# Gathering a decoder's chosen tokens on TensorE: transpositions with a permutation against fp32 products

## The chip, the core and the metric

The kernel runs on one core of one Trainium2 chip. The core has TensorE (PE, matrix products into PSUM), VectorE (DVE), ScalarE (ACT), GpSimd (POOL) and SyncE (SP), which here issues the DMA transfers. The metric is the device time of one execution in microseconds, less is better; a time is the median of several runs.

## The reference

Two decoder layers on 32 sequences of 100 tokens with 256 features, each sub-block followed by a layer norm: an agent attention, a cross attention on a context of 361 rows, an attention over chosen tokens, a windowed self attention, a second cross attention, and a quantised linear layer. The change touches the third:

```
gate = sigmoid(x @ Wg)                 # one number per token
_, idx = top_k(gate, 50)               # half of the 100 tokens
attn_in = x[idx]
q, k, v = attn_in @ Wq, attn_in @ Wk, attn_in @ Wv     # 16 heads of 16
o = softmax(q k^T / 4) v @ Wo
out = zeros; out[idx] = o * gate[idx]
x = layernorm(x + out)
```

## The kernel before

Sequences are worked on in pairs (NB = 2, so 200 tokens), 16 pairs in all. Four streams A to D hold a pair each, with tiles and two PSUM banks of their own (`bk[0]`, `bk[1]`), and take four turns (TURNS = 4). Each stream goes through the stages mix, first (cross attention), pick (the chosen tokens), local, second and quant. For each engine, a generator per stream issues a short piece of work and yields; the strings in `ORDER` say, letter by letter, whose piece comes next. So each engine works through a fixed list in which the four streams are interleaved, and waits on semaphores that the other engines raise. Ahead of the turns comes a stage over all sequences (`tensor_agents` and its like), which transposes all tokens at L355.

The stage pick in `tensor_turns`, `scalar_turns` and `vector_turns` goes like this, for one pair:

- DVE forms the gate logits (L1008), ACT the exponential (L748), DVE the gates (L1012, L1014): one column of 100 for each sequence.
- PE spreads the gates of a sequence over 100 partitions, so that each token sees all gates in its row: L514, a product of the gate column, broadcast to 100 columns, with the identity.
- DVE counts, for each token, the gates above its own (and equal ones of earlier tokens): its rank, 0 to 99 (L1019, L1023). Then it compares the rank with `slots` (L1027). `slots` has 128 columns for a sequence: those of its own half hold 0 to 49, all others -1. The result `pick` is a 100x128 matrix with a one where a token goes to a slot; slots of the first sequence are columns 0 to 49, of the second 64 to 113.
- PE gathers: L521 multiplies the tokens (100x128 of a feature half c, as weights) by `pick`, sums both sequences in PSUM, and so has the chosen tokens as columns. L525 transposes `pick` (for the way back).
- ACT copies the gathered columns to `xT` (L751 in the code; the trace gives all such copies the helper's line, L693) and the transposed `pick` to `pickT`.
- PE projects to q and k (L436) and v (L540), forms the scores of 16 heads (L557), transposes the exponentials (L566, 8 for a pair) and the spread reciprocals (L581, 2 for a pair), forms the head outputs (L577) and the output projection (L441), and scatters the rows back by products with `pickT` (L589). DVE multiplies by the gate and adds the residual (L1076).

An fp32 matrix product is issued as one call and stands in the trace as two matmuls; a transposition (`e.transpose`) stands as one. L431 is the transposition of tokens that opens the other stages, L471 and L632 are transpositions of exponentials (L632, 32 for a pair), L478 is the product with the context.

Of the kernel before, what the change touches and what calls it, by code (L numbers as in the profile page):

```python
# [9 lines left out]
ALU = mybir.AluOpType  # L10
# [3 lines left out]
B, S, D, S2 = 32, 100, 256, 361  # L14
H, DH = 16, 16
P = 128
NC = D // P
NB = 2
T = NB * S
# [4 lines left out]
CAP = S // 2  # L24
assert NB * CAP == S
HALF = P // NB
# [94 lines left out]
def program(nc, ins, out):  # L121
    ctx = ExitStack()
    with ctx:
        def sb(name, shape, dt=F32):
            return ctx.enter_context(nc.sbuf_tensor(name, list(shape), dt))
# [9 lines left out]
        ident = sb("ident", [P, P])  # L135
# [1 line left out]
        ones = sb("ones", [P, S])  # L137
        minus_half = sb("minus_half", [P, NB])
        before = sb("before", [S, S])
        slots = sb("slots", [S, NB, P])  # L140
        own = sb("own", [P, 2])
        heads = sb("heads", [P, 4])
        band_w = sb("band_w", [NM, S], BF16)
# [17 lines left out]
        class Stream:  # L161
            def __init__(s, n):
                s.n, s.name = n, "ABCD"[n]
                s.x = sb(f"x{n}", [P, NB, D])
                s.ctx = sb(f"ctx{n}", [P, NB, S2C, D])
                s.ctxT = sb(f"ctxT{n}", [P, NB, NC, S2])
                s.res = sb(f"res{n}", [P, NB, D])
                s.xplus = sb(f"xplus{n}", [P, NB, D])

                s.work = sb(f"work{n}", [P, HQ * S + NB * D])  # L170
                s.prod = s.work[0:S, HQ * S:HQ * S + NB * D].rearrange("p (b d) -> p b d", b=NB)
                s.p = s.work[0:S, 0:NB * S2C * P].rearrange("p (b k) -> p b k", b=NB)
                s.e = s.work[0:S, 0:HQ * S].rearrange("p (h k) -> p h k", h=HQ)
                s.e_pick = s.work[:, 0:H * HALF].rearrange("p (n j k) -> p n j k", n=H // 2, j=2)
                s.fo = s.work[:, HQ * S:HQ * S + D]
                s.rspread_pick = s.work[:, H * HALF:H * HALF + D]
                s.yq = s.work[0:S, 0:D].bitcast(BF16).rearrange("p (b d) -> p b d", b=NB)

                s.eT = sb(f"eT{n}", [P, HQ * S])
                s.pT = s.eT[:, 0:NB * S2C * S].rearrange("p (b j t) -> p b j t", b=NB, j=S2C)  # L180
                s.agent = s.eT[0:S, HQ * S - NB * D:].rearrange("p (b d) -> p b d", b=NB)
                s.yT = s.eT[:, 0:T].bitcast(BF16)[:, 0:NC * T].rearrange("p (c t) -> p c t", c=NC)
                s.tie = s.eT[0:S, 0:T].rearrange("p (b t) -> p b t", b=NB)
                s.pick = s.eT[0:S, T:T + NB * P].rearrange("p (b m) -> p b m", b=NB)
                s.xT = sb(f"xT{n}", [P, NC, T])
                s.aT = sb(f"aT{n}", [P, NC, T])
                s.qT = sb(f"qT{n}", [P, NC, T])
                s.kT = sb(f"kT{n}", [P, 2, NC, T])


                k_rows = s.kT[:, :, :, :].rearrange("p j c t -> p (j c t)")
                s.keys = [k_rows[:, 0:4 * S], s.work[:, HQ * S:HQ * S + 4 * S], k_rows[:, 4 * S:8 * S],
                          s.res[:, :, :].rearrange("p b d -> p (b d)")[:, 0:4 * S]]
                s.lm = s.kT[0:S, :, :, :].rearrange("p j c t -> p (j c t)")[:, 0:NB * S2].rearrange("p (b k) -> p b k", b=NB)
                s.v = sb(f"v{n}", [P, NB, H, 2 * DH])
                s.v_pick = sb(f"vs{n}", [P, NB, H // 2, 2 * DH])
                s.pickT = sb(f"pickT{n}", [P, NB, S])
                s.qbias = sb(f"qb{n}", [S, NB])
                s.bn = sb(f"bn{n}", [S, NB, 6])
                s.mv = sb(f"mv{n}", [S, NB, 2])  # L200
                s.vare = sb(f"ve{n}", [S, NB])
                s.rstd = sb(f"rstd{n}", [S, NB])
                s.mx = sb(f"mx{n}", [P, H])
                s.den = sb(f"den{n}", [P, H])
                s.rden = sb(f"rden{n}", [P, H])
                s.nbias = sb(f"nb{n}", [S, NB])
                s.sum = sb(f"sum{n}", [S, NB])
                s.rsum = sb(f"rsum{n}", [S, NB])
                s.z = sb(f"z{n}", [S, NB])
                s.ez = sb(f"ez{n}", [S, NB])  # L210
                s.gp = sb(f"gp{n}", [S, NB])
                s.gate = sb(f"gate{n}", [S, NB])

                s.shift = s.ez
                s.nmean = s.gp
                s.rank = sb(f"rank{n}", [S, NB])
                s.ms = sb(f"ms{n}", [S, NB])
                s.rms = sb(f"rms{n}", [S, NB])
                s.amax = sb(f"am{n}", [S, NB])
                s.am2 = sb(f"am2{n}", [S, NB])  # L220
                s.sc = sb(f"sc{n}", [S, NB])
                s.os = sb(f"os{n}", [S, NB])
                s.load_x = Loaded(sem(f"load_x{n}"), 1)
                s.load_agent = Loaded(sem(f"load_agent{n}"), 1)
                s.load_ctx = Loaded(sem(f"load_ctx{n}"), 2)
                s.load_mask = Loaded(sem(f"load_mask{n}"), 2)
                s.stored = Loaded(sem(f"stored{n}"), 1)
                s.tensor, s.scalar, s.vector, s.gpsimd = (
                    {stage: Steps(sem(f"{engine}_{stage}{n}"), names) for stage, names in stages.items()}
                    for engine, stages in (("tensor", TENSOR), ("scalar", SCALAR), ("vector", VECTOR), ("gpsimd", GPSIMD)))  # L230
# [60 lines left out]
        ld_w0, ld_wk, ld_c, ld_first, ld_const = (sem(n) for n in ("ld_w0", "ld_wk", "ld_c", "ld_first", "ld_const"))  # L291
# [130 lines left out]
        def tensor_turns(e, s):  # L422
            bk = [psum[:, NB * s.n + b, :] for b in range(NB)]
# [68 lines left out]
            for t in range(TURNS):  # L492
# [18 lines left out]
                    e.wait_ge(ld_const, LD_CONST)  # L511
                e.wait_ge(*dve("gt", t))
                for b in range(NB):
                    last = e.matmul(bk[0][0:S, b * S:(b + 1) * S], s.gate[:, b:b + 1].to_broadcast([S, S]), ident[0:S, 0:S],  # L514
                                    start=True, stop=True)
                last.then_inc(*pe.up("gates"))
                yield
                e.wait_ge(*dve("pk1", t))
                for c in range(NC):
                    for b in range(NB):  # L520
                        last = e.matmul(bk[0][:, c * P:(c + 1) * P], s.x[0:S, b, c * P:(c + 1) * P], s.pick[:, b, :],  # L521
                                        start=b == 0, stop=b == NB - 1)
                last.then_inc(*pe.up("gath"))
                for b in range(NB):
                    last = e.transpose(bk[1][:, b * S:(b + 1) * S], s.pick[:, b, :], ident[0:S, 0:S])  # L525
                last.then_inc(*pe.up("selT"))
                yield
                e.wait_ge(*act("xT", t))
# [57 lines left out]
                yield  # L586
                e.wait_ge(*act("fo", t))
                for b in range(NB):
                    e.matmul(bk[b][0:S, 0:D], s.pickT[HALF * b:HALF * (b + 1), b, :], s.fo[HALF * b:HALF * (b + 1), :],  # L589
                             start=True, stop=True).then_inc(*pe.up(f"sc{b}"))  # L590
                yield

# [96 lines left out]
        def scalar_turns(e, s):  # L689
            bk = [psum[:, NB * s.n + b, :] for b in range(NB)]  # L690

            def copy(dst, src, **kw):
                return e.activation(dst, src, ACT.Copy, **kw)  # L693
# [46 lines left out]
            for t in range(TURNS):  # L740
# [7 lines left out]
                e.activation(s.ez[:, :], s.z[:, :], ACT.Exp, scale=-1.0).then_inc(*act.up("ez"))  # L748
                yield
                e.wait_ge(*pe("gath", t))  # L750
                copy(s.xT[:, :, 0:P], bk[0][:, 0:NC * P].rearrange("p (c m) -> p c m", c=NC)).then_inc(*act.up("xT"))  # L751
                e.wait_ge(*pe("selT", t))
                copy(s.pickT[:, :, :].rearrange("p b t -> p (b t)"), bk[1][:, 0:T]).then_inc(*act.up("selT"))
                yield
# [4 lines left out]
                e.wait_ge(*pe("v", t))  # L759
                if t == 0:  # L760
                    e.wait_ge(*s.gpsimd["start"]("zeros"))
                copy(s.v_pick[0:HALF, :, :, 0:DH],
                     bk[0][0:HALF, 0:NB * P].rearrange("p (b n d) -> p b n d", b=NB, d=DH)).then_inc(*act.up("vs0"))
                yield
                for g in range(2):
                    e.wait_ge(*dve(f"su{g}", t))
# [160 lines left out]
        def vector_turns(e, s):  # L927
# [48 lines left out]
            for t in range(TURNS):  # L976
# [47 lines left out]
                                           ALU.is_gt, ALU.add, accum_out=s.rank[:, b:b + 1]).then_inc(*dve.up(f"rk{b}"))  # L1024
                for b in range(NB):
                    e.wait_ge(*dve(f"rk{b}", t))
                    e.tensor_scalar(s.pick[:, b, :], slots[:, b, :], s.rank[:, b:b + 1], None, ALU.is_equal).then_inc(  # L1027
                        *dve.up(f"pk{b}"))
                yield
                e.wait_ge(*pe("k", t))  # L1030
# [6 lines left out]
                e.wait_ge(*pe("v", t))  # L1037
                if t == 0:
                    e.wait_ge(*s.gpsimd["start"]("zeros"))
                e.tensor_copy(s.v_pick[HALF:P, :, :, DH:2 * DH],  # L1040
                              bk[0][HALF:P, 0:NB * P].rearrange("p (b n d) -> p b n d", b=NB, d=DH)).then_inc(*dve.up("vs1"))
                yield
                e.wait_ge(*pe("hs", t))
                def of_bank(stat, g):
# [241 lines left out]
        def sync_first(e):  # L1286
# [34 lines left out]
            for n, tile in (("ident_b", ident_b), ("before", before), ("own", own), ("heads", heads), ("band_w", band_w),  # L1321
                            ("band_x", band_x)):
                e.dma_start(tile[:, :], ins[n]).then_inc(ld_const, 16)
            e.dma_start(slots[:, :, :], ins["slots"]).then_inc(ld_const, 16)
            e.wait_ge(*agent_pe("u"))
            for s in (SC_, SD):
                load_ctx(e, s, 0)
# [110 lines left out]
def constants():  # L1438

    bf = mybir.dt.np(BF16)  # L1440
    t = np.arange(S)
    edge = np.concatenate([np.arange(NEDGE), np.arange(S - NEDGE, S)])
    one_key = (edge[:, None] == t[None, :]).astype(np.float32)
    mask = np.where(np.abs(edge[:, None] - edge[None, :]) > BAND, NEG, 0.0).astype(np.float32)
    slots = np.full((S, NB, P), -1.0, np.float32)
    for b in range(NB):
        slots[:, b, b * HALF:b * HALF + CAP] = np.arange(CAP)
    return {
        "ident": np.eye(P, dtype=np.float32), "ident_b": np.eye(P).astype(bf),
        "before": (t[None, :] < t[:, None]).astype(np.float32), "slots": slots,  # L1450
# [62 lines left out]
```

## Time and profile before

| | |
|---|---|
| median of 3 runs | 916.03 us (913.7, 916.03, 917.0) |
| span of the profiled execution | 917.6 us; what lies around it is not recorded |
| mean granted TensorE clock | 0.956 |
| busy: PE, DVE, ACT, POOL | 834.6, 674.2, 491.1, 361.5 us |
| PE matmuls | 7963 |
| moved by DMA | 53.34 MB, mean 58 GB/s |

The profiled execution's span lies 1.6 us above the median of the runs. Busy time of an engine is the time in which at least one of its instructions is under way; matmuls overlap, so their mean length (some 250 ns) is not what one costs. What one costs is read from where the next group begins, which is how the chain of waits counts a piece. "PEld" is the loading of weights, which runs beside the matmuls.

### The profile page before, as it was taken

Reading aid. Unit: us, or ns where it says so; the run is one execution under the profiler, and the core shown is the slowest. Engines: PE = TensorE matmul, PEld = TensorE weight load, DVE = VectorE, ACT = ScalarE, POOL = GpSimd, SP = SyncE. Lnnn points to the kernel's source line nnn. Section 1 sums busy time; section 2 is a strip of 40 time slices with the busy share of each in tenths; the row PEclk is TensorE's granted clock in tenths of the full one; section 3 lists DMA queues with packets and bytes.
Section 4 is the critical chain, followed back from the end, with each engine's and each line's share of the span. In section 5 each row is a group of like instructions: output and inputs, shape, how many; then the busy total and the mean of one; then the engine's idle time right before and its main releaser. Section 6 shows DMA issues by size and latency. Waiting matters only on the chain.

```text
span 917.6 us, 20617 instructions
## 1 busy us (share of the span) xinstructions
PE 834.6 (91%) x7963; PEld 629.7 (69%) x7963; DVE 674.2 (73%) x1973; ACT 491.1 (54%) x1509; POOL 361.5 (39%) x592
## 2 busy tenths in 40 slices
PE   8999999997879999998886699999889899999993
PEld 5567887675657787665665588766667688866772
DVE  5255887878776788796575678788678678788676
ACT  3135455765554544685454544577446454477654
POOL 0376222027756312215654632302567621210555
PEclk9989999999998999999998799999889799999996
DMA  7880000002262000001343000001142300000001
GB/s 231 265 319 24 1 2 1 2 27 68 74 218 84 10 2 1 1 2 52 101 179 118 19 10 2 1 2 27 53 160 98 108 10 2 1 2 2 2 1 36
DMA packets 22942, 53.34 MB, mean 58 GB/s; under 512 B 3656, under 2 KB 9548, under 8 KB 22844
## 3 DMA queue, kind: packets, MB, share of 16 engines
q1 hardware_dynamic: 22844, 52.02, 16.9%
q8 instruction: 63, 1.03, 0.5%
q14 instruction: 35, 0.29, 0.1%
HBM read 48.71 MB, written 3.31 MB: 57 GB/s over the span
## 4 chain that ended last, share of the span: by engine, by line
PE 47%; DVE 8%; POOL 7%; ACT 6%; DMA 3%; issue 2%; SPq 0%; ACTq 0%; DVEq 0%; POOLq 0%
PE psum L436 8%; PE psum L441 7%; PE psum L478 5%; PE psum L621 4%; PE psum L464 4%; PE psum L641 3%; PE psum L632 3%; POOL rstd L1190 2%; DMA out<-xplus 2%; ACT x L699 2%; PE psum L624 2%; PE psum L540 1%; PE psum L557 1%; PE psum L566 1%; PE psum L521 1%
## 5 line engine op out<-in xcount | busy, mean ns | idle before, releaser
L699 ACT ACTIVATE x<-res,ez,rstd 100x256 f32<-100x256 f32 x160 | 87.5, 597 | 76.7 <-POOL ez L1193 76.4
L478 PE MATMUL psum<-eT,ctx 128*128 128x100 f32 x768 | 103.7, 293 | 8.0 <-ACT eT L693 6.0
L478 PEld LDWEIGHTS psum<-eT,ctx 128*128 128x128 f32 x768 | 99.4, 208 | 11.7 <-ACT eT L693 6.2
L1188 POOL TENSOR_SCALAR ve<-mv 100x2 f32<-100x2 f32 x96 | 21.9, 228 | 182.1 <-DVE mv L936 178.3
L464 PE MATMUL psum<-ctxT,qT 128*100 128x361 f32 x256 | 88.9, 493 | 3.7 <-ACT qT L715 3.0
L801 ACT ACTIVATE work<-psum,mx 100x100 f32<-100x100 f32 x256 | 68.1, 366 | 32.3 <-DVE mx L1099 32.0
L1190 POOL TENSOR_TENSOR rstd<-ve,minus_half 100x2 f32<-100x2 f32 x96 | 75.2, 783 | 8.0
L693 ACT ACTIVATE eT<-psum 100x400 f32<-100x400 f32 (+3 forms) x128 | 61.1, 494 | 28.7 <-PE psum L471 13.1
L1172 POOL TENSOR_TENSOR kT<-cell,kT 100x722 f32<-100x722 f32 x12 | 20.6, 1716 | 135.1 <-ACT cell L673 135.1
L933 DVE BATCH_NORM_STATS2 bn<-res 100x6 f32<-100x256 f32 x192 | 71.2, 412 | 0.0
L807 ACT ACTIVATE work<-psum,mx 100x100 f32<-100x100 f32 x256 | 69.2, 390 | 2.8 <-DVE mx L1102 2.8
L693 ACT ACTIVATE xT<-psum 128x400 f32<-128x400 f32 (+2 forms) x80 | 35.9, 448 | 63.2 <-PE psum L521 26.5
L464 PEld LDWEIGHTS psum<-ctxT,qT 128*100 128x100 f32 x256 | 43.5, 176 | 36.1 <-issue 4.9
L632 PE MATMUL psum<-ident,work 100*100 100x100 f32 x512 | 61.6, 253 | 3.3 <-ACT work L807 2.8
L632 PEld LDWEIGHTS psum<-ident,work 100*100 100x100 f32 x512 | 48.6, 128 | 13.0 <-ACT work L807 5.3
L1109 DVE RECIPROCAL xT<-psum 128x100 f32<-128x100 f32 x64 | 49.6, 775 | 9.7 <-PE psum L641 8.6
L1193 POOL TENSOR_SCALAR ez<-mv,rstd 100x1 f32<-100x1 f32 x192 | 52.1, 287 | 9.5
L1099 DVE TENSOR_REDUCE mx<-psum 100x4 f32<-100x400 f32 x64 | 36.5, 570 | 19.7 <-PE psum L624 18.7
L471 PE MATMUL psum<-ident,work 100*128 100x100 f32 x192 | 28.0, 264 | 18.6 <-ACT work L728 17.9
L1207 POOL COPY work<-rden 128x256 f32<-128x256 f32 x16 | 6.3, 396 | 95.8 <-DVE rden L1061 95.8
L471 PEld LDWEIGHTS psum<-ident,work 100*128 100x128 f32 x192 | 21.1, 147 | 27.6 <-ACT work L728 24.8
L1106 DVE COPY eT<-psum 100x400 f32<-100x400 f32 x64 | 35.7, 564 | 5.5 <-PE psum L632 5.3
(241 smaller groups left out, 2087.0 us busy)
## 6 DMA issues: line engine op xcount, KB each, us to landing
ctx<-in_ctx SPq DMA_DIRECT2D x16, 768.0 KB, 7.6
ctxT<-in_ctxT SPq DMA_DIRECT2D x16, 722.0 KB, 5.7
cell<-in_cell SPq DMA_DIRECT2D x12, 282.0 KB
seq<-in_seq SPq DMA_DIRECT2D x12, 282.0 KB
x<-in_x SPq DMA_DIRECT2D x16, 200.0 KB
out<-xplus SPq DMA_DIRECT2D x16, 200.0 KB
eT<-agent_rows SPq DMA_DIRECT2D x12, 200.0 KB
work<-in_x SPq DMA_DIRECT2D x4, 400.0 KB
```

The lines of the kernel that those rows point to most:

```text
L436: last = e.matmul(dst, w[:, c, h * P:(h + 1) * P], n(c), start=c == 0, stop=c == NC - 1)
L441: last = e.matmul(dst, xT(c), w[:, c, :], start=c == 0, stop=c == NC - 1)
L464: last = e.matmul(bk[b][0:S, 0:S2], s.qT[:, c, b * S:(b + 1) * S], s.ctxT[:, b, c, :], start=c == 0, stop=c == NC - 1)
L478: last = e.matmul(bk[b][:, c * S:(c + 1) * S], s.ctx[:, b, j, c * P:(c + 1) * P], s.pT[:, b, j, :], start=j == 0, stop=j == S2C - 1)
L632: last = e.transpose(bk[g][0:S, q * S:(q + 1) * S], s.e[:, 4 * g + q, :], ident[0:S, 0:S])
L693: return e.activation(dst, src, ACT.Copy, **kw)
L699: e.activation(dst[0:S, b, :], s.res[0:S, b, :], ACT.Identity, scale=s.rstd[:, b:b + 1], bias=s.shift[:, b:b + 1]).then_inc(*act.up(f"x{b}"))
L801: last = e.activation(s.e[:, h, :], bk[0][0:S, h % 4 * S:(h % 4 + 1) * S], ACT.Exp, bias=s.mx[0:S, h:h + 1])
L807: last = e.activation(s.e[:, h, :], bk[1][0:S, h % 4 * S:(h % 4 + 1) * S], ACT.Exp, bias=s.mx[0:S, h:h + 1])
L933: e.bn_stats(s.bn[:, b, :], s.res[0:S, b, :]).then_inc(*dve.up(f"bn{b}"))
L1190: e.tensor_tensor(s.rstd[:, :], s.vare[:, :], minus_half[0:S, 0:NB], ALU.pow).then_inc(*pool.up("rstd"))
L1193: e.tensor_scalar(s.shift[:, b:b + 1], s.mv[:, b, 0:1], s.rstd[:, b:b + 1], -1.0, ALU.mult, ALU.mult).then_inc(*pool.up(f"nm{b}"))
```

## The change

Three things. The gates are spread by transpositions in place of products. `slots` becomes one 100x100 matrix whose rows are 0 to 99, so `pick` holds, for each sequence, the permutation by all 100 ranks; the gather becomes a transposition of the tokens with this permutation as its moving operand, for each sequence and feature half apart, 100 columns each. What follows takes the first 64 ranks of each sequence where it took the 64 slots before; rows 50 to 63 of a half now hold tokens that weren't chosen, in place of zeros, so v and the scatter are cut to 50 rows. The transposition of `pick` for the way back reads 128 columns that begin at 0 or 36, so that the second sequence's ranks fall on partitions 64 to 113 as before. The order of the instructions on each engine, their waits and their number of calls stay the same.

```diff
-        slots = sb("slots", [S, NB, P])
+        slots = sb("slots", [S, S])
...
-                s.pick = s.eT[0:S, T:T + NB * P].rearrange("p (b m) -> p b m", b=NB)
+                s.pick = s.eT[0:S, T:T + NB * S].rearrange("p (b m) -> p b m", b=NB)
+                s.pick_rows = [s.eT[0:S, T + b * (S - HALF):T + b * (S - HALF) + P] for b in range(NB)]
...
-                    last = e.matmul(bk[0][0:S, b * S:(b + 1) * S], s.gate[:, b:b + 1].to_broadcast([S, S]), ident[0:S, 0:S],
-                                    start=True, stop=True)
+                    last = e.transpose(bk[0][0:S, b * S:(b + 1) * S], s.gate[:, b:b + 1].to_broadcast([S, S]), ident[0:S, 0:S])
...
-                        last = e.matmul(bk[0][:, c * P:(c + 1) * P], s.x[0:S, b, c * P:(c + 1) * P], s.pick[:, b, :],
-                                        start=b == 0, stop=b == NB - 1)
+                        at_ = (c * NB + b) * S
+                        last = e.transpose(bk[0][:, at_:at_ + S], s.x[0:S, b, c * P:(c + 1) * P], s.pick[:, b, :])
                 last.then_inc(*pe.up("gath"))
                 for b in range(NB):
-                    last = e.transpose(bk[1][:, b * S:(b + 1) * S], s.pick[:, b, :], ident[0:S, 0:S])
+                    last = e.transpose(bk[1][:, b * S:(b + 1) * S], s.pick_rows[b], ident[0:S, 0:S])
...
-                    e.matmul(bk[b][0:S, 0:D], s.pickT[HALF * b:HALF * (b + 1), b, :], s.fo[HALF * b:HALF * (b + 1), :],
+                    part = slice(HALF * b, HALF * b + CAP)
+                    e.matmul(bk[b][0:S, 0:D], s.pickT[part, b, :], s.fo[part, :],
...
-                copy(s.xT[:, :, 0:P], bk[0][:, 0:NC * P].rearrange("p (c m) -> p c m", c=NC)).then_inc(*act.up("xT"))
+                copy(s.xT[:, :, 0:P].rearrange("p c (b m) -> p c b m", b=NB),
+                     bk[0][:, 0:NC * T].rearrange("p (c b t) -> p c b t", c=NC, b=NB)[:, :, :, 0:HALF]).then_inc(*act.up("xT"))
...
-                copy(s.v_pick[0:HALF, :, :, 0:DH],
-                     bk[0][0:HALF, 0:NB * P].rearrange("p (b n d) -> p b n d", b=NB, d=DH)).then_inc(*act.up("vs0"))
+                copy(s.v_pick[0:CAP, :, :, 0:DH],
+                     bk[0][0:CAP, 0:NB * P].rearrange("p (b n d) -> p b n d", b=NB, d=DH)).then_inc(*act.up("vs0"))
...
-                    e.tensor_scalar(s.pick[:, b, :], slots[:, b, :], s.rank[:, b:b + 1], None, ALU.is_equal).then_inc(
+                    e.tensor_scalar(s.pick[:, b, :], slots[:, :], s.rank[:, b:b + 1], None, ALU.is_equal).then_inc(
...
-                e.tensor_copy(s.v_pick[HALF:P, :, :, DH:2 * DH],
-                              bk[0][HALF:P, 0:NB * P].rearrange("p (b n d) -> p b n d", b=NB, d=DH)).then_inc(*dve.up("vs1"))
+                e.tensor_copy(s.v_pick[HALF:HALF + CAP, :, :, DH:2 * DH],
+                              bk[0][HALF:HALF + CAP, 0:NB * P].rearrange("p (b n d) -> p b n d", b=NB, d=DH)).then_inc(*dve.up("vs1"))
...
-    slots = np.full((S, NB, P), -1.0, np.float32)
-    for b in range(NB):
-        slots[:, b, b * HALF:b * HALF + CAP] = np.arange(CAP)
+    slots = np.broadcast_to(t.astype(np.float32), (S, S))
```

## Rows read from the trace of the kernel before

**Rows 1.** The page, section 1: busy time, share of the span, instructions.
```profile
span 917.6 us, 20617 instructions
PE 834.6 (91%) x7963; PEld 629.7 (69%) x7963; DVE 674.2 (73%) x1973; ACT 491.1 (54%) x1509; POOL 361.5 (39%) x592
```
**Rows 2.** The page, section 2: tenths in 40 slices of 22.9 us.
```profile
PE   8999999997879999998886699999889899999993
...
PEclk9989999999998999999998799999889799999996
```
**Rows 3.** Busy time of each engine in four windows over the stage pick.
```profile
core 0: us, PE busy (x) PEld busy (x) DVE busy (x) ACT busy (x) POOL busy (x), PEclk, DMA share, GB/s
95.00:150.00 55.00, 53.97 (x652) 45.18 (x652) 45.55 (x146) 26.36 (x71) 15.70 (x32) 1.00 0.01 2
315.00:370.00 55.00, 54.37 (x617) 44.01 (x617) 45.56 (x137) 25.58 (x71) 12.72 (x30) 1.00 0.01 2
540.00:590.00 50.00, 49.42 (x582) 40.95 (x581) 42.17 (x128) 23.86 (x66) 10.46 (x24) 1.00 0.01 2
750.00:805.00 55.00, 54.70 (x609) 44.39 (x609) 45.95 (x142) 27.03 (x77) 9.99 (x25) 1.00 0.01 2
```
**Rows 4.** Pieces of the chain that ended last: start us, us, what.
```profile
537.28 0.53 PE psum L514 x4
...
540.24 0.91 PE psum L521 x8
...
541.17 0.39 ACT xT L693
...
545.58 0.35 PE psum L514 x4
...
552.62 1.10 PE psum L521 x8
...
561.36 1.09 PE psum L521 x8
562.45 0.17 PE psum L525 x2
...
566.34 0.59 PE psum L566 x4
...
568.89 0.34 PE psum L431 x4
...
577.12 0.50 PE psum L431 x4
...
794.85 0.69 PE psum L632 x8
```
**Rows 5.** By source line: duration ns min/median/max, first and last start, forms; who waited.
```profile
L514 PE MATMUL psum<-ident,gate x64: 249/252/487, 91.5 to 770.7; 100*100 100x100 f32 x64
...
  DVE eT L1019: 4.3, 7
...
L521 PE MATMUL psum<-eT,x x128: 272/275/377, 99.8 to 774.0; 100*128 100x128 f32 x128
...
  ACT xT L693: 26.5, 11
...
L525 PE MATMUL psum<-ident,eT x32: 249/249/249, 100.7 to 774.2; 100*128 100x100 f32 x32
...
L431 PE MATMUL psum<-ident,x x192: 247/249/427, 59.4 to 878.2; 100*128 100x100 f32 x192
```
**Rows 6.** By source line L1027, DVE's comparison with the slots, and who waited.
```profile
L1027 DVE TENSOR_SCALAR eT<-slots,rank x32: 277/281/303, 93.0 to 772.1; 100x128 f32<-100x128 f32 x32
...
  PEld psum L521: 1.0, 4
```
**Rows 7.** Windows of the early stage and of two clock levels, columns as in rows 3.
```profile
9.00:26.00 17.00, 17.00 (x112) 9.87 (x116) 10.52 (x59) 7.38 (x16) 0.00 (x0) 1.00 0.87 266
...
290.00:295.00 5.00, 5.00 (x26) 4.69 (x27) 2.96 (x11) 2.19 (x6) 2.41 (x5) 0.59 0.28 84
...
320.00:325.00 5.00, 5.00 (x64) 4.49 (x63) 4.17 (x18) 1.86 (x6) 0.00 (x0) 1.00 0.01 3
```
**Rows 8.** By source line L355, the early transpositions, columns as in rows 5.
```profile
L355 PE MATMUL psum<-ident,ctx x16: 374/374/429, 16.3 to 20.1; 100*128 100x100 f32 x16
```
**Rows 9.** Pieces of the chain at either level of the clock.
```profile
290.48 2.65 PE psum L478 x12
...
324.76 1.32 PE psum L478 x12
```

More of the change, by code:

```diff
@@ L1323, in sync_first @@
                 e.dma_start(tile[:, :], ins[n]).then_inc(ld_const, 16)
-            e.dma_start(slots[:, :, :], ins["slots"]).then_inc(ld_const, 16)
+            e.dma_start(slots[:, :], ins["slots"]).then_inc(ld_const, 16)
             e.wait_ge(*agent_pe("u"))
```

## Prediction

> **What bounds the kernel now.** I read the page first. TensorE (PE) is busy for 91% of the span and the next engine, VectorE (DVE), for 73% [rows 1]. A mean over stages decides nothing, so the 40 slices come next: PE stands at 9 in most of them and dips at regular places, four of them (with the last slices), while the granted clock is at full speed outside these dips [rows 2]. The dips are where a turn of the four streams ends and the next begins. The change sits in the stage "pick", which runs once in each turn, between the dips. So I asked for four windows that cover it: together 215 us, in which PE is busy for 212.5 us, DVE for 179.2 us, ACT for 102.8 us, at clock 1.00 and next to no DMA, summed over the four rows [rows 3]. PE is busy for 98.8% there, DVE for 83%.
>
> Busy is not yet bound, so the fourth view is the chain that ended last. Between 540 and 580 us it runs through PE piece after piece, the groups that the change touches among them, and leaves PE for a copy of ACT here and there [rows 4]. That is the reading on which the forecast stands: in this stage a piece of PE's time is a piece of the run's time. The chain as listed begins at 237 us; for the first turn I rely on its window alone, which looks like the others [rows 3].
>
> **The change part by part.** One fact first: an fp32 product is two matmuls in the trace, a transposition one. The gates are 2 products for each of 16 pairs, and the source view lists 64 matmuls; the gather is 4 products for each pair, and lists 128; the transposition of the pick matrix is 2 for each pair and lists 32 [rows 5].
>
> *Gates.* Two products, 4 matmuls, take 0.35 us of the chain (0.53 us where the next group follows badly) [rows 4]. What two transpositions take comes from the nearest rows: eight 100x100 ones in a row took 0.69 us, 0.086 us each; two of the pick matrix took 0.17 us, 0.085 each [rows 4]. That makes 0.17 us for the gates, so 0.18 us less for each pair.
>
> *Gather and the transposition behind it.* The 8 matmuls of the gather took 0.91, 1.10 and 1.09 us in three places, mean 1.03, and the two transpositions behind them 0.17: together 1.20 us [rows 4]. Afterwards there are 4 + 2 transpositions of 100 columns. The form of the four (tokens as weights 100x128, 100 columns moving) is the one with which the kernel transposes its tokens for every other stage: four took 0.34 us [rows 4]. Six at 0.086 are 0.52 us, so 0.68 us less.
>
> Sum: 0.18 + 0.68 = 0.86 us for each pair, times 16 = **13.8 us** of PE's time. The best case takes the 1.10 us gather: 0.93 us for a pair, 14.9 us. The other end takes the dearer transpositions of the trace: four of the same form once took 0.50 us, 0.125 each, and four of 128 columns 0.59 us, 0.148 each [rows 4]. With 0.125: gates 0.25 against 0.35, the rest 0.75 against the cheaper 0.91 + 0.17, so 0.43 for a pair and 6.9 us in all. With 0.148: 0.05 + 0.19 = 0.24, 3.8 us. I take 0.086 because six in a row have only one place where a different group follows, and form and neighbour match the rows at 0.34 and 0.17.
>
> The Trainium skill ("TensorE: Matmul & The Clock Gate", section Terms) says that transpose mode makes FP32 four times faster. By that rule against the pair of passes the gates would fall from 0.35 to some 0.09 us and the gather from 1.03 to some 0.26, an estimate of 16.5 us in all. The rows disagree: a transposition costs as much as one pass, not a half of one, so the sum stays with the rows.
>
> *ACT's copy of the gathered tokens* still writes 256 elements of 128 partitions, out of four pieces of 64 now. It took 0.39 us in the chain [rows 4]; I cost the pieces at nothing, with 0.1 us for each pair (1.6 us) as the other bound. It matters only where it is exposed, and 11 times ACT sat waiting for the gather, 26.5 us in all [rows 5], so an earlier gather lets it start earlier. Nothing is queued anew: instruction order, semaphores and waits of every queue stay as they are.
>
> *DVE's comparison with the slots* goes from 128 to 100 elements, 281 ns now [rows 6], twice for each pair. A fall in proportion would be 60 ns, 2 us of DVE in all; a fixed part may leave nothing. PE waited for it at four places only, 1.0 us together [rows 6], so I count zero. Copies of 50 partitions instead of 64, the scatter's contraction over 50 rows instead of 64, and one smaller constant load cost what they did: the columns that stream through are the same, and the load is early. Its ends are a gain of 0 to 1.0 us, that wait as a whole.
>
> *What is given back.* The PE pieces leave a stage where DVE is busy for 83% of the time. With 3.4 us less for each turn of some 54 us, DVE goes to 88%. Some of the removed time was cover for a result that is then late. The first suspect is the copy of the gathered tokens, for which the query projection waits: 0.39 us and 0.06 of handover. In one kind of place the chain runs through this copy already, so the full gain of the gather counts; in the other, PE has work of another stream in between and the cover stays. What is late next is DVE's work: sums, reductions and softmax of pick, which PE's transpositions wait for. I take a quarter, 3.4 us; none and a half (6.9 us) are the bounds. A quarter because DVE has a sixth of its time free and PE has next to none, which puts it nearer to none.
>
> So 13.8 - 3.4 = 10.4 us less. Against the profiled span, 917.6 us [rows 1], that is 907.2 us. The median of the three runs is 916.03 us, 1.6 below this span, so the forecast for the median is **905.6 us**.
>
> **The rivals.**
>
> A. DVE takes over. Half of the gain turns into waits: 13.8 - 6.9 = 6.9 us, 909.1 us. For it: DVE at 83% in a fixed order, with seven waits for the gates, 4.3 us in all [rows 5], so the two engines hand over often. Against it: the chain between 540 and 580 us hardly touches DVE.
>
> B. Transpositions at 0.125 us: 6.9 us of PE, a quarter given back, 5.2 us less, 910.8 us. For it: the 0.50 us row. Against it: rows at 0.34, 0.69 and 0.17.
>
> C. Slower, by the clock. From 9 to 26 us PE is busy without a gap, with transpositions and narrow products, and one transposition takes 374 ns where the same form takes 249 later [rows 5, 7, 8]. The records show 1.00 for that window, but the durations are those of 1.2 GHz. So a PE that is always busy, much of it with transpositions, did not run at 2.4 GHz. The change raises the share of transpositions in pick: 12 to 18 for each pair. If the clock fell to its lower level, the price is in the chain: 12 context matmuls took 2.65 us at the low level and 1.32 us at the high one [rows 7, 9], so every 5 us at the low level cost 2.5. The point from which it decides is 10.4 / 2.5, about four such stretches, one for each turn; with two for each turn the loss is 20 and the time 916.0 + 9.6 = 925.6 us. Against it: the local stage issues 32 transpositions for each pair at full clock, and in pick the products of four streams are woven between.
> The Trainium skill ("TensorE: Matmul & The Clock Gate", Part 4: PE-mode transpose) states this as a rule: transposes do not count as activity for the clock. The early window agrees with it; the four pick windows, at 1.00 with a dozen transpositions for each pair in them, show that products near them suffice.
>
> D. Next to nothing: the transposition with a permutation as its moving operand is executed as two passes like the product, or the time comes back in full at the turn's end, where PE waits for others anyway. Then only the narrower gather is left, under 2 us: some 915 us. Against the first: every transposition in the trace is one matmul. Against the second: the streams' work at the turn's end starts from results of this stage, so all of it shifts.
>
> **How the numbers follow.** Forecast 0.70, A 0.10, B 0.08, C 0.05, D 0.07. The bound for "same" is 0.5%, 4.6 us, about what a measurement of this kernel can tell from no change. Faster: all of the forecast, 0.09 of A and 0.05 of B = 0.84. Same: 0.01 of A, 0.03 of B, D = 0.11. Slower: C = 0.05. The range: 14.9 us less with nothing given back is 901.1, and the runs scatter by 1 or 2 us, so 900; above, B with half given back is 3.5 us less, 912.5, and some scatter, so 913. C and D lie outside.
>
> **What would show it.** The gates should read x32 and the gather x64, near 249 ns each with 100 columns; in the chain the gates' pieces near 0.17 us and the gather's near 0.34. PE's busy time should fall by some 14 us or more and the pick windows should end earlier by 2 to 3 us a turn, adding up from turn to turn. The clock row in these windows should stay at 9s. Wrong would be: x64 and x128 again (D), a clock under 1.00 inside pick (C), DVE pieces in the chain where PE's stood (A), or four transpositions at 0.50 us (B).

## The result and the profile after

The changed kernel took 911.94 us in the median of 20 runs, against 916.89 for the kernel before in the same rounds. These medians lie 5.0 us apart. The ratio is 0.9924, with a 95% interval from 0.9903 to 0.9944: 7.0 us less, 5.1 to 8.9. The ratios aren't formed from these medians, and leave out runs counted as slow, here one of 1316.64 us of the kernel before and the changed kernel's two longest, of 917.84 and 918.69 us (with these two kept in, the means differ by 5.6 us). The forecast was 10.4 less (905.6), the range 900 to 913. The changed kernel was run twice more later, beside other kernels (e8, e10): ratios 0.9901 and 0.9892, some 9 and 10 us less. So the time fell as predicted and lies in the range, and by each of these measures the gain is smaller than the forecast.

The page of the changed kernel, its head and the clock in 40 slices, against [rows 1, 2]:

```profile
span 914.6 us, 20425 instructions
PE 825.1 (90%) x7867; PEld 618.9 (68%) x7867; DVE 673.7 (74%) x1973; ACT 488.9 (53%) x1509; POOL 362.3 (40%) x592
...
PEclk9989899999998999999998799999999899999996
```

PE has 96 matmuls fewer, as counted, and DVE is as busy as before. By source line, the gates and the gather, against [rows 5]:

```profile
L515 PE MATMUL psum<-ident,gate x32: 247/250/406, 92.9 to 768.5; 100*100 100x100 f32 x32
...
L522 PE MATMUL psum<-eT,x x64: 247/249/429, 101.0 to 771.2; 100*128 100x100 f32 x64
...
  DVE eT L1029: 2.3, 7
```

The change does what it says: 32 and 64 instead of 64 and 128. Two things are to be seen beside that. The longest matmul of the gather took 429 ns, where the longest was 377 before and 306 in the changed kernel's second profile: some of this profile ran at the lower clock. (The gates had such a one before, of 487 ns.) And PE now waits for DVE's comparison with the ranks (L1029) seven times, 2.3 us, where it waited four times, 1.0 us [rows 6]. The chain between 550 and 566 us (start us, us, what), against [rows 4]:

```profile
555.91 0.51 PE psum L522 x4
556.42 0.02 issue
556.44 0.39 ACT xT L694
...
561.50 0.17 PE psum L515 x2
...
564.04 0.49 PE psum L522 x4
564.53 0.17 PE psum L525 x2
```

The gates cost 0.17 us where they cost 0.35, as forecast. The gather costs 0.51 and 0.49 us where the same two groups cost 1.10 and 1.09: 0.6 less, not 0.75. A piece of the chain runs from the end of the group before to its own end, so it holds the gap ahead of its first matmul, in the product as in the transposition. From the start of a group to the start of the next one, by the timelines of the kernel before and of e8 (the changed kernel again), the four transpositions take 0.34 or 0.40 us, near the forecast's 0.34, and the products took 0.89 or 0.99. Over all 16 pairs the gather falls from 15.0 to 6.0 us and the gates from 7.1 to 4.0. So PE loses 12.2 us in all, 3.0 for each turn (forecast 13.8).

Where did 12.2 turn into 7? The cleanest ruler is the time between the starts of the same two PE groups at either end of the stage in each turn. For the first turn, from the timelines of the kernel before, of the changed kernel, and of the changed kernel's second profile (e8):

```profile
86.50 0.48 PE L471 MATMUL psum<-ident,work 100*128 100x100 f32 x3 [0.42 <-ACT work L728]
...
149.28 1.62 PE L436 MATMUL psum<-xT,a_q 128*128 128x200 f32 x8
```
```profile
87.91 0.31 PE L472 MATMUL psum<-ident,work 100*128 100x100 f32 x1 [0.41 <-ACT work L729]
...
151.86 1.62 PE L437 MATMUL psum<-xT,a_q 128*128 128x200 f32 x8
```
```profile
86.94 0.48 PE L472 MATMUL psum<-ident,work 100*128 100x100 f32 x3 [0.41 <-ACT work L729]
...
148.57 1.62 PE L437 MATMUL psum<-xT,a_q 128*128 128x200 f32 x8
```

62.78 us before, 63.95 in the changed kernel's first profile, 61.63 in its second. Measured in this way in all profiles but e1's (us from start to start, the same groups everywhere; before: 86.50 to 149.28, 296.52 to 355.09, 516.84 to 588.79, 723.79 to 789.98):

```
                                  turn 1  turn 2  turn 3  turn 4
before                             62.78   58.57   71.95   66.19
changed                            63.95*  56.63   68.89   63.64
e8, changed again                  61.63   56.64   69.21   63.67
e10, changed, third                61.63   58.31*  69.16   63.74
e2, gather only                    62.04   56.89   69.32   62.39
e3, products of 100 columns        62.65   58.48   71.51   65.93
e4, first turn products            62.66   56.63   69.07   64.51
e5, gather issued twice            62.88*  57.47   70.05   63.03
e6, a wait for each sequence       63.85*  56.53   69.00   61.82
e11, e6 again                      61.64   56.53   69.23   64.32
e7, gather put first               61.92   56.61   69.75   64.54
e9, e6 with first turn products    62.46   56.54   68.99   63.89
e13, short search for equals       61.24   56.39   69.11   64.22
* the clock fell inside this stretch
```

The first three columns repeat to 0.3 us where the clock holds. In e4, e6, e7, e11 and e13 the first 0.7 to 1.7 us of turn 3 are at the low clock too; e11, with 1.7, has e8's time all the same. The fourth column begins in a fall of the clock that every kernel has, and scatters by over 2, because the part of that fall that lies in the stretch differs: 7.2 us before, 6.1 in e8, 7.8 in e4, 0.2 in e2 and e6. In e8 the four stretches gain 1.15, 1.93, 2.74 and 2.52 us: 8.3 us of the 12.2. The last of these owes a part to the clock: e4, which is the changed kernel in turn 4 and has 0.6 us more of the low clock than the kernel before, gains 1.68 there. With that the sum is 7.5. As for the stars, set against the same turn of e8 (for e6, of e11), the falls cost 2.3 us in the changed kernel's turn 1, 2.2 in e6's and 1.7 in e10's turn 2. e5's turn 1 is 1.25 us longer than e8's, of which its added work makes 0.8 in turns 2 and 3, which leaves some 0.4 for its fall.

The windows around the first turn's fall, first of the changed kernel's first profile, then of its second (columns as in rows 3):

```profile
105.00:110.00 5.00, 3.79 (x52) 2.61 (x48) 4.87 (x27) 1.69 (x6) 0.00 (x0) 0.83 0.01 3
110.00:115.00 5.00, 5.00 (x26) 4.67 (x26) 3.60 (x9) 1.49 (x4) 0.00 (x0) 0.50 0.00 0
```
```profile
105.00:110.00 5.00, 3.49 (x54) 2.95 (x55) 4.87 (x24) 1.36 (x5) 0.00 (x0) 1.00 0.01 3
110.00:115.00 5.00, 4.70 (x60) 4.03 (x58) 4.60 (x16) 2.33 (x7) 0.40 (x1) 1.00 0.00 0
```

The same program, the same gap on PE near 105 us (DVE is busy for 4.87 of 5 us there), and once the clock falls to 0.50 for 6.8 us (a third of the first window, all of the second), so that 26 matmuls start from 110 to 115 us instead of 60; once it does not.

What is given back can be read from PE's waits in the stretches of e8 for turns 2, 3 and 4 (294 to 352, 514 to 583 and 715 to 779 us; waiter, releaser, us, times, longest). One wait is there in all three and in none of them before:

```profile
PE psum L472 <- ACT work L729: 0.2, 1, 0.2
```
```profile
PE psum L472 <- ACT work L729: 0.3, 1, 0.3
```
```profile
PE psum L472 <- ACT work L729: 0.5, 1, 0.5
```

L472 transposes the exponentials of another stream's cross attention, and in PE's order it comes soon behind a gather. The longer gather used to cover ACT's exponential (L729); the shorter one doesn't. In turn 3 ACT had itself waited for DVE (L955) just before this exponential; in turns 2 and 4 it came from work of its own.

### The profile page after: what moved, and what is told of

Same layout as the page of the kernel before. It is cut to its first block, busy times and chain, and to the rows that moved or that the text cites. A ratio compares the mean times of both kernels' runs of the same rounds, so it can differ in the third digit from the quotient of the medians.

```text
span 914.6 us, 20425 instructions
## 1 busy us (share of the span) xinstructions
PE 825.1 (90%) x7867; PEld 618.9 (68%) x7867; DVE 673.7 (74%) x1973; ACT 488.9 (53%) x1509; POOL 362.3 (40%) x592
## 4 chain that ended last, share of the span: by engine, by line
PE 43%; DVE 11%; POOL 7%; ACT 6%; DMA 4%; issue 2%; SPq 1%; DVEq 0%; ACTq 0%; POOLq 0%
PE psum L437 8%; PE psum L442 7%; PE psum L479 6%; PE psum L622 4%; PE psum L633 3%; PE psum L642 3%; PE psum L465 2%; DMA out<-xplus 2%; POOL rstd L1192 2%; ACT x L700 2%; PE psum L625 2%; DVE bn L935 2%; DMA seq<-in_seq 1%; PE psum L540 1%; POOL xplus L1199 1%
## 5 line engine op out<-in xcount | busy, mean ns | idle before, releaser
L472 PE MATMUL psum<-ident,work 100*128 100x100 f32 x192 | 28.6, 266 | 21.7 <-ACT work L729 21.2
L472 PEld LDWEIGHTS psum<-ident,work 100*128 100x128 f32 x192 | 21.1, 147 | 31.6 <-ACT work L729 28.8
```

## The experiments

**e1: gates only.** The kernel before with the first edit of the diff alone:

```diff
-                    last = e.matmul(bk[0][0:S, b * S:(b + 1) * S], s.gate[:, b:b + 1].to_broadcast([S, S]), ident[0:S, 0:S],
-                                    start=True, stop=True)
+                    last = e.transpose(bk[0][0:S, b * S:(b + 1) * S], s.gate[:, b:b + 1].to_broadcast([S, S]), ident[0:S, 0:S])
```

> Only the gates are spread by transpositions; the gather stays a product. Theory 1 (PE's pieces have the forecast size, about a quarter is given back to waits, and the first turn's pick stage loses its gain to a fall of the clock that sparser PE work brings): the gates' groups fall from 0.35-0.45 us to 0.18-0.27, 16 x 0.2 = 3.2 us of PE, so 2 to 3 us less than before, 914 to 915; no clock fall near 108 us, since the gather stays dense. Theory 2 (no clock part: DVE takes half of any gain in all turns): 1 to 2 us less.

Ratio 0.9979 (0.9952 to 1.0006), 1.9 us less. The interval holds both theories and zero. Its profiled execution took 1424.6 us and is used for nothing here, so whether its clock fell near 108 us isn't known.

**e2: gather only.** The changed kernel with the gates as products again.

> Gather by transpositions, gates by products. Theory 1: 16 x 0.57 = 9.1 us of PE; three turns give three quarters of their share, 5.1 us less, the first turn between 1.5 us less and 1 us more, as its clock falls or not: 911 to 912. A clock under 1.00 between 105 and 120 us in the profile if the transpositions of the gather bring the fall. Theory 2: half of 9.1, 912.3, and clock 1.00 there.

Ratio 0.9943 (0.9921 to 0.9964), 5.2 us less. The clock stayed at 1.00 from 95 to 150 us; turns 1 to 3 gained 0.74, 1.68 and 2.63 us. So the gather makes most of the gain, and the gates add 0.41, 0.25 and 0.11 in these turns (e8 against e2), which fits the 0.2 us for each pair only in part: 0.8 us a turn left PE. Its turn 4 can't be compared, as most of the fall of the clock lies ahead of the stretch.

**e3: the layout without the transpositions.** In the changed kernel:

```diff
-                        last = e.transpose(bk[0][:, at_:at_ + S], s.x[0:S, b, c * P:(c + 1) * P], s.pick[:, b, :])
+                        last = e.matmul(bk[0][:, at_:at_ + S], s.x[0:S, b, c * P:(c + 1) * P], s.pick[:, b, :],
+                                        start=True, stop=True)
```

> The changed kernel's layout (100 ranks, one gather per sequence and feature half, 100 columns) with products in place of all transpositions. It takes out what the operation's kind does and keeps the rest. Both theories: the gather's groups cost 8 passes near 0.10 us, 0.8 to 0.9 us, so 0 to 2 us less than before: 915 to 917. Were layout and copies the source of the gain, it would come near 912.

Ratio 1.0017 (0.9986 to 1.0048): no gain. Its gather groups in the chain:

```profile
552.42 1.08 PE psum L523 x8
...
561.13 1.06 PE psum L523 x8
```

1.08 and 1.06 us with 100 columns, against 1.10 and 1.09 with 128: the columns are worth next to nothing here, the kind of the operation is worth all. That is a little more than the second pass. From start to start the 128 matmuls of e3's gathers take 14.7 us, 0.115 each, and e8's 64 transpositions of the same shape 6.0 us, 0.094 each; their weights load in 140 ns where e3's take 192. ACT's copy in four pieces and the narrower comparison on DVE don't show either.

**e4: products in the first turn alone.** `e.transpose` where `t` is above 0, else `e.matmul` as in e1's minus lines and e3's plus lines.

> The changed kernel, but in the first turn gates and gather are products as in e3; turns 2 to 4 are as changed. Theory 1: the first turn gave no gain and often a fall of the clock; with the products back its clock stays 1.00 between 100 and 120 us and the time is 1 to 3 us below the changed kernel's, 909 to 911. Theory 2: a turn's gain is lost, 1.7 us, so 913 to 914.

Ratio 0.9918 (0.9893 to 0.9944), 7.5 us less. It has the first turn of before (62.66) and the later turns of the changed kernel. The clock held. The number can't be told from the changed kernel's three (0.9924, 0.9901, 0.9892): giving up a first turn that gains 1.15 and sometimes loses 2.3 changes next to nothing.

**e8: the changed kernel again.**

> The changed kernel again, for a second profile. Theory 1a (the fall of the clock near 108 us belongs to the change, since the first turn's pick is sparse on PE): clock under 1.00 between 105 and 120 us again, and a first turn that gains nothing. Theory 1b (the fall comes in some executions only): clock 1.00 there, the first turn gains 0.5 to 1 us and the profile's span is 2 to 3 us under the first profile's 914.6. Either way turns 2 to 4 gain 1.9 to 2.9 us each in pick, and the median is 910 to 913.

Ratio 0.9901 (0.9875 to 0.9927), and theory 1b holds: clock 1.00, 61.63 us, a span of 906.3. The rest of the difference to 914.6 lies between the stages, where the clock falls in every profile, before too [rows 2], at places and for lengths that vary.

**e5: the gather issued twice.**

```diff
-                for c in range(NC):
+                for c in list(range(NC)) * 2:
```

> The changed kernel with the four gathering transpositions of each pair issued twice, into the same place: 64 more at 0.086 us, 5.5 us of PE. Theory 1 (about a quarter of what leaves PE in this stage returns as waits): 4 to 5 us more than the changed kernel, 916. Theory 2 (DVE bounds the stage by now, more PE work hides beside it): 0 to 2 us more.

Ratio 0.9938 (0.9907 to 0.9970): 3.4 us more than e8 by the ratios, with overlapping intervals. The stretches are sharper: turns 2 and 3 are 0.83 and 0.84 us longer than e8's, of 1.4 us that PE got (four pairs, four transpositions of 0.086). Some 60% arrives, less than theory 1's three quarters and more than theory 2 allows. PE still bounds the stage, not alone.

**e6: a wait for each sequence.**

```diff
-                e.wait_ge(*dve("pk1", t))
-                for c in range(NC):
-                    for b in range(NB):
+                for b in range(NB):
+                    e.wait_ge(*dve(f"pk{b}", t))
+                    for c in range(NC):
```

> The changed kernel, but PE waits for the first sequence's permutation, transposes its two halves, and only then waits for the second's. The changed kernel's PE waits 2.3 us in all for the comparisons with the ranks, the kernel before 1.0. If what is given back sits in this wait, 1 to 2 us less than the changed kernel; if it is spread over other waits, within 0.5 us of it.

Ratio 0.9881 (0.9852 to 0.9911), the lowest of all, 906.2 us. But its turns 2 and 3 (56.53, 69.00) are those of the changed kernel within 0.2, and its first turn has a fall of the clock. So it was run again.

**e11: e6 again, e10: the changed kernel beside it.**

> e6 again, beside the changed kernel. If its lead of 2 us holds (part of what is given back sits in PE's wait for both permutations), 0.987 to 0.990 of the kernel before and 1 to 2 us under e10; if it was scatter, within 0.5 us of e10.

> The changed kernel a third time, on the chip and in the rounds of e9 and e11, as their measure: 0.990 to 0.993 of the kernel before. Its profile adds one more look at 105 to 120 us.

e11 0.9913 (0.9878 to 0.9947), e10 0.9892 (0.9857 to 0.9927). The lead was scatter. The wait for the second sequence is not where the gain is held. e10's profile brought a fall of the clock in turn 2 instead, of 3.4 us. There it begins behind a wait of PE for ACT's copy in the stage first, at the low clock from the group on that follows:

```profile
312.68 2.91 PE L437 MATMUL psum<-xT,x_k 128*128 128x200 f32 x8 [1.75 <-ACT xT L694]
```

The same wait stands there in e8 (1.76 us) and before (1.61 us), and the clock held.

**e7: the gather put first.** In PE's order list, four places, one for each turn, such as

```diff
-        "ABABDADDDDDAACBABACABABBBCDBDBCABCACACACDCCDCBADABDBDBDCBADADDBACCACDBABCDBCDDCABDCBCDAADCBCDADABDAB"
+        "ABABDADDDDDAACBABACABABBBCDBDBCABCACACACDCCDCBADABDBDBDCBADADDBCACACDBABCDBCDDCABDCBCDAADCBCDADABDAB"
```

> The changed kernel with PE's order altered in four places, in one for each turn: the gather goes ahead of the other stream's piece that stood before it, so that PE has 0.5 to 0.9 us of work while ACT copies the gathered tokens (PE waits 0.30 us there in each of the four now). Theory 1 (PE bounds pick): 1 to 1.5 us less than the changed kernel. Theory 2 (DVE bounds): no difference, or a little more, as the piece put off is late for DVE.

Ratio 0.9947 (0.9919 to 0.9975). Turn 2 is as it was (56.61), turn 3 half a microsecond longer. Theory 2's outcome, but the timelines show another road to it than a bound DVE. In turn 3 the wait of 0.30 us for the gathered tokens is gone, as meant. The scores of the other stream (L557) now come behind the gather; ACT, which takes its work in a fixed order too, waits 1.31 us for DVE's work on them (L1053), its copy of q comes late behind that, and PE waits 0.81 us for it before L540, where e8 has no wait. Filling a wait of PE buys nothing when the piece that was put off is late for its own reader.

**e9: e6 and e4 together.**

> e6 (a wait for each sequence's permutation) with the products of e4 in the first turn. Two theories of the fall of the clock near 108 us: if it is chance in any kernel, this lies within 1 us of e6, or 1 us above, as the first turn's gain of up to 1.2 us is given up; if it comes with the first turn's transpositions (seen in three of six profiles that have them, in none of three without), the clock stays 1.00 there and the two effects nearly cancel: within 1 us of e6, with less scatter.

Ratio 0.9908 (0.9878 to 0.9939), clock 1.00 in the pick windows. Within the expected microsecond or so of the others, and so undecided.

**e13: less work for DVE.** The search for equal gates runs over 2 columns and isn't added to the rank. (In a first form, e12, the rank added a constant triangle instead, so that `pick` was no permutation; there is no time for it.)

```diff
-                    e.scalar_tensor_tensor(s.tie[:, b, :], bk[0][0:S, b * S:(b + 1) * S], s.gate[:, b:b + 1], before[:, :],
+                    e.scalar_tensor_tensor(s.tie[:, b, 0:2], bk[0][0:S, b * S:b * S + 2], s.gate[:, b:b + 1], before[:, 0:2],
...
-                    e.scalar_tensor_tensor(s.tie[:, b, :], bk[0][0:S, b * S:(b + 1) * S], s.gate[:, b:b + 1], s.tie[:, b, :],
-                                           ALU.is_gt, ALU.add, accum_out=s.rank[:, b:b + 1]).then_inc(*dve.up(f"rk{b}"))
+                    e.scalar_tensor_tensor(s.tie[:, b, :], bk[0][0:S, b * S:(b + 1) * S], s.gate[:, b:b + 1], ones[0:S, :],
+                                           ALU.is_gt, ALU.mult, accum_out=s.rank[:, b:b + 1]).then_inc(*dve.up(f"rk{b}"))
```

> The changed kernel with DVE's search for equal gates of earlier tokens cut from 100 columns to 2, in all turns, and left out of the rank: the order among exactly equal gates is not settled. DVE loses 8 times some 0.15 us for each turn, 1.1 us. In the first turn DVE is busy for 11.6 of 12 us around 106 us: if it bounds that stretch and holds back the first turn's gain, the first turn comes out 0.7 to 1.2 us shorter than the changed kernel's (1.15 us gained where the clock did not fall), and turns 2 to 4, where PE bounds, 0 to 0.4 us each; in all 1 to 2 us less than the changed kernel. If DVE does not bound the first turn either, nothing there, and the small first gain has another cause.

Ratio 0.9923 (0.9892 to 0.9955). The instruction fell from 314 to 211 ns, 0.8 us a turn and not 1.1; the first turn became 0.39 us shorter (61.24), the second 0.25, the third 0.10. So DVE holds back a part of the first turn's gain, and about half of what was taken off it arrives, in line with PE's wait for the ranks there, which falls from 0.6 to 0.4 us. The rest of what is given back lies in other handovers, as PE's waits in that stretch of e8 show (92 to 150 us: waiter, releaser, us, times, longest):

```profile
PE psum L557 <- ACT vs L694: 0.8, 1, 0.8
PE psum L522 <- DVE eT L1029: 0.6, 1, 0.6
PE psum L540 <- ACT qT L694: 0.3, 1, 0.3
PE psum L437 <- ACT xT L694: 0.3, 1, 0.3
```

Before, the same stretch has 0.4 us for the first, none for the second and third, and the same 0.3 for the fourth: 1.3 us of waits are new, 0.9 of them on results that had been ready in time.

## Why the prediction was right, and where its sizes were off

- **PE bounds the stage.** Right for the greater part. Of the 3.0 us that left PE in each turn, 2.7 arrive in turn 3, 1.9 in turn 2 and 1.7 to 2.5 in turn 4, and what e5 puts back arrives for 60%.
- **One pass for two.** Right, and e3 shows that the kind of the operation is the whole of the gain. Rival D is out: each transposition with a permutation is one matmul. The rule of the Trainium skill on a fourfold speed ("TensorE: Matmul & The Clock Gate", section Terms) would have given near 0.26 us for a gather, by the prediction's estimate from 1.03 us in the chain; the changed kernel's chain has 0.49 and 0.51.
- **The sum, 13.8 us.** The gates' term held (0.18 us forecast, 0.19 measured for each pair). The gather's was too high: 0.69 us for each pair forecast, 0.57 measured. It set a price with the gap ahead of the first matmul (1.03 us in the chain) against one without it (0.34). Measured sum 12.2, inside the stated 3.8 to 14.9. The sign of rival B did come, pieces of 0.50 us in the chain, but not its price: the products' pieces hold the same gap, so 12.2 us left PE and not 6.9.
- **A quarter given back.** Mis-sized: 3.9 of 12.2 us by e8's stretches, a third, and 4.7 with e4's turn 4. The prediction named one share for all turns; it is nine tenths that arrive in turn 3, six in turn 2, six to eight in turn 4, and under four in turn 1. The first suspect, ACT's copy of the gathered tokens, had no new part in it: that wait is 0.3 us before and after. New are, in turn 1, waits for DVE's comparison, for the copy of q and for that of v, and in turns 2 to 4 the wait for ACT's exponentials, where the prediction expected DVE's sums. The mechanism, cover that is gone, was right; the result that is late was another.
- **Rival A.** Its 6.9 us less can't be told from the 7.0 of the ratio by the time alone. Against it stand the stretches, in which less than half is given back, and the waits of turns 2 to 4, which are mostly for ACT. For it stands e13, by which DVE holds back a part of turn 1.
- **The first turn "looks like the others".** This is the step that failed. The prediction took it from a window of 55 us, 83% for DVE. Turn 1 arrives with 1.15 us of 3.0. Between 100 and 112 us DVE is busy for 11.5 us of 12, and there two streams' gates stand one behind the other, which in later turns lie 8 us or more apart. A full DVE is not enough of a reason, though. In turn 3 of the kernel before it is as full, around the gather that begins at 561 us, whose 0.6 us arrived in full:

```profile
555.80:567.80 12.00, 12.00 (x160) 9.80 (x162) 11.47 (x40) 5.43 (x16) 1.83 (x5) 1.00 0.01 3
```

  PE has no idle time there, while between 100 and 112 us it is busy for 11.05 us of 12 and has waits of its own already. Why the two places differ was not tested.
- **Rival C, the clock.** If it held, then in a small form that the text had not priced. It expected falls in every turn or none. The runs show a fall in the first turn of 3 of the 9 profiles whose first turn gathers by transpositions (6.8 us long in two, 3.4 in e5), and in none of the 4 whose first turn uses products. Three of nine against none of four can be chance. Whether transpositions count less as activity, as the Trainium skill has it ("TensorE: Matmul & The Clock Gate", Part 4: PE-mode transpose), or whether PE's larger gaps do it, was not separated: the changed kernel had the same gap with and without a fall. In turns 3 and 4 no profile shows one beyond the fall with which the turn begins; the one in turn 2 stands behind a wait between products that other executions have without a fall. The early window, on which the rival leaned, doesn't bear it out either. Its 1.00 is no measurement, as the kernel before has no clock record ahead of 34.7 us. And in e4, e9 and e11 the same early transpositions took 249 or 250 ns in the median and not 374, so they can run at the higher clock, there with waits for transfers between them (e4, against [rows 8]):

```profile
L356 PE MATMUL psum<-ident,ctx x16: 249/249/307, 14.0 to 17.0; 100*128 100x100 f32 x16
```

- **The total.** The four stretches together are 6.4, 8.3 and 6.6 us shorter than before in the changed kernel's three profiles, 7.1 on average. Outside them the first profile is 3.3 us longer than before, the second 2.9 shorter and the third the same. That the record's 7.0 is so close to the stretches' 7.1 is luck; the three measurements of this kernel spread over 3 us.
- **Better versions.** None. e4, e6, e7, e9 and e13 lie between 0.988 and 0.995, around the changed kernel's 0.989 to 0.992, and e6's lead did not repeat.

## What to carry to other kernels

An fp32 product whose one operand holds a single one in each row and column can be issued as a transposition, and costs one pass instead of two; narrowing its columns from 128 to 100 was worth next to nothing beside that. When pricing a piece, take both prices from the same ruler: both with the gap ahead of the first matmul, or both without. Before pricing what a bound engine loses, look behind each piece that shrinks, turn by turn, for the result that its successor needs: how much of it was covered decides how much of the gain arrives, here nine tenths in one turn and under four in another. And when the whole time scatters by as much as the effect, measure the stage from group start to group start, which repeated to 0.3 us here where the runs' medians moved by 3.

## What the runs showed of the hardware

- A transposition with a permutation other than the identity as its moving operand takes what one with the identity takes: median 249 ns (L522), as for the same form with the identity before (L525, L431), at one matmul each.
- The weights of a transposition load faster than those of a product of the same shape. Gates, 100x100, in the profiles before and after:

```profile
L514 PEld LDWEIGHTS psum<-ident,gate x64: 162/167/287, 91.4 to 770.6; 100*100 100x100 f32 x64
```
```profile
L515 PEld LDWEIGHTS psum<-ident,gate x32: 121/125/203, 92.8 to 768.4; 100*100 100x100 f32 x32
```

The gather's, 100x128, load in 192 ns as a product (e3) and in 140 as a transposition.

- The same program with the same gap on PE kept its clock in one execution and lost it for 6.8 us in another, so a single profile can't show whether a change brings such a fall.
